# Rows turned by VectorE and exchanged in SBUF, and new orders in two stages of a four-layer graph network

## What is computed

```
x = _layernorm(x + L0(x))   # relu([x, max over edges of x[dst] - x[src]] @ W + b)
x = _layernorm(x + L1(x))   # silu(x @ lin), two convs with edge sums, cat, three residual layers, norm
x = _layernorm(x + L2(x))   # degree-normed sum of x @ W over edges and loops, relu
x = _layernorm(x + L3(x))   # weighted edge sum, layer norm, relu
```

## Time and profile before

| | |
|---|---|
| time, median of 3 runs | 5421.13 us (5409.99 to 5424.0) |
| the profiled execution's own time | 5410.58 us |
| its span, first to last instruction | 5408.9 us |
| busy: TensorE, VectorE, ScalarE, GpSimd | 78%, 79%, 67%, 75% of the span |
| TensorE's mean granted clock | 0.863 |

### The profile page before, as it was taken

The page is one execution under the profiler, slowest core; times in us unless marked ns, Lnnn a source line. Parts: engine busy times, 40 slices in busy tenths (PEclk is TensorE's granted clock), DMA queues, the critical chain, the costliest instruction groups (busy, mean ns, idle before and its releaser), DMA issues. The chain is left out here.

```text
span 5408.9 us, 82889 instructions
## 1 busy us (share of the span) xinstructions
PE 4223.2 (78%) x18435; PEld 2618.7 (48%) x18558; DVE 4247.1 (79%) x8746; ACT 3645.5 (67%) x9127; POOL 4062.4 (75%) x4129
## 2 busy tenths in 40 slices
PE   6999999999999978999999888888576745551000
PEld 3555555555555533444444588887454534440000
DVE  7888888888888746788788799999788854457776
ACT  3777777777777635666666688888688854446665
POOL 6788888888888777777777177777777767777777
PEclk9999999999999989999999999999655567665555
DMA  6877787777777646777777699999798967774443
GB/s 181 206 208 205 204 200 205 208 204 199 209 205 203 163 106 202 208 203 205 207 202 207 207 383 376 377 378 374 272 281 280 285 196 227 229 242 152 135 135 104
DMA packets 850458, 1213.29 MB, mean 224 GB/s; under 512 B 347599, under 2 KB 517001, under 8 KB 850215
## 3 DMA queue, kind: packets, MB, share of 16 engines
q1 hardware_dynamic: 744566, 1059.81, 61.4%
q0 software_dynamic: 100352, 149.23, 12.7%
q10 hardware_dynamic: 5296, 1.73, 0.1%
HBM read 648.60 MB, written 438.76 MB: 201 GB/s over the span
## 5 line engine op out<-in xcount | busy, mean ns | idle before, releaser
L847 ACT ACTIVATE p_s<-p_ps,cols 128x512 f32<-128x512 f32 x588 | 404.5, 688 | 341.1 <-PE p_ps L801 216.7
L729 POOL DMA_INDIRECT home<-edge_row_cols,scatter_cols x392 | 447.1, 1141 | 119.3 <-issue 119.3
L198 POOL DMA_INDIRECT out<-u_res,scatter_cols x392 | 407.7, 1040 | 121.7 <-issue 118.4
L1196 POOL DMA_INDIRECT ring_rows<-t_rows,home_cols x384 | 409.1, 1065 | 119.2 <-issue 88.5
L191 POOL DMA_INDIRECT u_rows<-t_rows,home_cols x392 | 388.2, 990 | 145.5 <-issue 117.3
L191 POOL DMA_INDIRECT ring_rows<-t_rows,home_cols x400 | 396.7, 992 | 126.3 <-issue 114.7
L722 POOL DMA_INDIRECT p_xs<-in_x,src_cols x388 | 387.0, 997 | 123.3 <-issue 117.0
L722 POOL DMA_INDIRECT p_xd<-in_x,dst_cols x388 | 398.3, 1027 | 107.2 <-issue 107.2
L1205 POOL DMA_INDIRECT home_cols<-home,src_cols x376 | 368.1, 979 | 144.2 <-issue 86.0
L212 DVE BATCH_NORM_STATS2 r_counts<-r_v 128x6 f32<-128x256 f32 x980 | 373.4, 422 | 11.0 <-issue 0.9
L227 ACT ACTIVATE r_x<-r_v,r_nm,r_rs 128x128 f32<-128x128 f32 x784 | 321.8, 482 | 83.0 <-DVE r_nm L1773 83.0
(11 more groups left out here) (307 smaller groups left out, 13894.1 us busy)
## 6 DMA issues: line engine op xcount, KB each, us to landing
ring_rows<-in_x SPq DMA_DIRECT2D x98, 512.0 KB, 6.2
p_xT<-p_xt SPq DMA_DIRECT2D x392, 128.0 KB
t_rows<-p_o SPq DMA_DIRECT2D x98, 512.0 KB
p_x1T<-p_oT SPq DMA_DIRECT2D x392, 128.0 KB
hT<-ring_own SPq DMA_DIRECT2D x98, 512.0 KB
q_hn<-hT SPq DMA_DIRECT2D x98, 512.0 KB
r_h<-hT SPq DMA_DIRECT2D x98, 512.0 KB
r_x<-t_rows SPq DMA_DIRECT2D x98, 512.0 KB
```

Of the source, the lines that this page charges most:

```text
L198: nc.gpsimd.indirect_dma_start(out=table, out_offset=bass.IndirectOffsetOnAxis(ap=idx[:, j:j + 1], axis=0), in_=rows[:, j, :], in_offset=N ...
L729: nc.gpsimd.indirect_dma_start(out=tab["home"], out_offset=bass.IndirectOffsetOnAxis(ap=s["scat"][:, k:k + 1], axis=0), in_=s["at"][:, k:k ...
L847: nc.scalar.activation(act_out[i][:, :], flat(bank_r if i else bank_t), ACT.Silu, bias=col(LS0 + i)).then_inc(r_act[i], 1)
L1196: nc.gpsimd.indirect_dma_start(out=rows[:, e % 4, j, :], out_offset=None, in_=tab["t1"], in_offset=bass.IndirectOffsetOnAxis(ap=s["home"][ ...
```

## The change

In `setup`, a second half of layer 0's weights is loaded with its rows in the squares' order (`w1_swapped`), and `wsum` is the sum of the two swapped halves, made after the last weights have landed.

In `nodes01`:

- The target rows of an edge block are no longer turned by TensorE and copied by ScalarE. VectorE turns them in squares into one buffer (`p_xdt`), SyncE exchanges them with four DMAs of 64 KB into `p_xdT`, whose runs are 32 elements (128 bytes) long, and the edge products read that.
- TensorE's node products of layer 0 (794) move ahead of the two root products (784, 787).
- VectorE's line 952 moves behind the norm statistics of the step and behind residual 1; the new turning stands right after it.
- On GpSimd, four of the last index gathers (`homes(3)`) move behind the gathers of the first two edge blocks of the next stage.

In `edges1`:

- SyncE's loop first stores the finished block, loads the `ends` rows and issues the exchange `q_xT`, and then does the dense loads and the rest. The two loads of the `home` table move behind the first exchange.
- Residual product 0 goes to the bank `bank_t` in place of `bank_r`, so that it does not wait for ScalarE's read of residual product 2; that wait moves to residual product 1.

```diff
+                e = t // 2 - 1 - BEHIND
+                if live(e, EB):
+                    sp.wait_ge(xd_squared, e + 1)
+                    after(sp, e_product, e - 1)
+                    swap_groups(sp, xdT[:, e % 2].rearrange("p j a i -> p a j i"), xd_turned[:, :, :], xdT_in[e % 2])
...
-            homes(3)
...
+            homes(3)
...
+                if t.live(NB):
+                    q = t.pair()
+                    pe.wait_ge(xT_in[q.of(2)], landed(2, q, 4))
+                    after(pe, biased, t.b)
+                    for j in range(G):
+                        i = nc.tensor.matmul(bank_o[:, j, :], xT[:, q.of(2), j, :, :, t.slot % 2].rearrange("p a i -> p (a i)"), first["w0"][:, :],
+                                             start=True, stop=True)
+                    i.then_inc(product, 1)
                 n = t.back(7)
...
-                    pe.wait_ge(xd_copied, e.b + 1)
+                    pe.wait_ge(xdT_in[e.of(2)], landed(2, e, 4))
...
-                if even and e.live(EB):
-                    pe.wait_ge(xd_in[e.of(2)], landed(2, e, G))
-                    after(pe, xd_copied, e.b)
-                    transpose4(nc, bank_t, xd[:, e.of(2)], s["ident"]).then_inc(xd_turned, 1)
...
-                    nc.scalar.activation(xdT[:, e.of(2), :], flat(bank_t), ACT.Copy).then_inc(xd_copied, 1)
...
+                if even and e.live(EB):
+                    dve.wait_ge(xd_in[e.of(2)], landed(2, e, G))
+                    if e.past(1):
+                        dve.wait_ge(xdT_in[e.back(1).of(2)], landed(2, e.back(1), 4))
+                    turn_squares(nc, xd_turned[:, :, :].rearrange("p c (j i) -> p c j i", j=G), xd[:, e.of(2)]).then_inc(xd_squared, 1)
...
             for t in range(EB + 10):
+                e = t - 6
+                if live(e, EB):
+                    sp.wait_ge(r_added[2], e + 1)
+                    sp.dma_start(tab["eT"][e], hs[3][:, e % 4, :]).then_inc(h_saved[e % 4], DMA)
...
+                if t % 2 == 0 and live(t, EB):
+                    q = t // 2
+                    sp.wait_ge(squared, t + 2)
+                    after(sp, lined_g, t - 2)
+                    swap_groups(sp, xT[:, q % 2], squares[:, q % 2], xT_in[q % 2])
...
-                    after(pe, r_act[2], n.b)
-                    nc.tensor.matmul(flat(bank_r), s["lins"][:, 0, :], hs[0][:, n.of(2), :],
+                    if t.fixed and t.b == MASK_AT + 1:
+                        pe.wait_ge(copied, 2)
+                    nc.tensor.matmul(flat(bank_t), s["lins"][:, 0, :], hs[0][:, n.of(2), :],
...
                     pe.wait_ge(r_added[0], n.b + 1)
+                    after(pe, r_act[2], n.b)
```

More of the change, by code:

```diff
@@ L582, in nodes01 @@
         act_out = [sb(f"p_s{i}", [P, BLK]) for i in range(3)]
-        run, xdT = sb("p_run", [P, 2, BLK]), sb("p_xdT", [P, 2, BLK])
+        run, xd_turned, xdT = sb("p_run", [P, 2, BLK]), sb("p_xdt", [P, 4, BLK // 4]), sb("p_xdT", [P, 2, G, 4, 32])
         ve, oe, oeT = sb("p_ve", [P, 2, G, H]), sb("p_oe", [P, 2, G, H]), sb("p_oeT", [P, 2, BLK])
@@ L598, in nodes01 @@
         x_squared, xT_in = sem("x_squared"), [sem(f"xT_in{i}") for i in range(2)]
+        xd_squared, xdT_in = sem("xd_squared"), [sem(f"xdT_in{i}") for i in range(2)]
         (product, biased, summed, counted, guarded, rooted, scaled,
@@ L788, in step @@
                                      start=True, stop=True).then_inc(u_done2, 1)
[L789 to L796, removed]
                 n = t.back(8)
@@ L962, in step @@
                     residual(1, n)
+                q = t.pair().back(1)
+                if even and q.live(QB):
+                    lo, hi = batch(q)
+                    dve.wait_ge(rooted, q.b + 1)
+                    after(dve, applied, 2 * (q.b - 1), NB)
+                    after(dve, e_applied, q.b - 1 - BEHIND)
+                    nc.vector.scalar_tensor_tensor(nm[:, q.of(2), lo:hi], st[:, q.of(2), lo:hi, MEAN_OF], -1.0,
+                                                   rs[:, q.of(2), lo:hi], ALU.mult, ALU.mult).then_inc(scaled, 1)
+                if even and e.live(EB):
[3 more added lines that the diff above has]
+                    turn_squares(nc, xd_turned[:, :, :].rearrange("p c (j i) -> p c j i", j=G), xd[:, e.of(2)]).then_inc(xd_squared, 1)
                 if not even and e.live(EB):
@@ L1132, in _ @@
             home_v = tab["home"].rearrange("(b p h) o -> p b (h o)", p=P, h=2 * G)
-            for c in range(NC):
-                sp.dma_start(home[:, c].rearrange("p (b h) j -> p b (h j)", h=2),
-                             home_v[:, c * NB // 4:(c + 1) * NB // 4, :]).then_inc(home_in[c], DMA)
             for t in range(EB + 10):
+                e = t - 6
+                if live(e, EB):
+                    sp.wait_ge(r_added[2], e + 1)
+                    sp.dma_start(tab["eT"][e], hs[3][:, e % 4, :]).then_inc(h_saved[e % 4], DMA)
+                e = t - 3
+                if e % 2 == 0 and live(e, EB):
+                    after(sp, masked, e - 2)
+                    load_row_pair(sp, ends[:, e % 4:e % 4 + 2, :], tab["ends"], e // 2, ends_in[e // 2 % 2])
+                if t % 2 == 0 and live(t, EB):
[3 more added lines that the diff above has]
+                    swap_groups(sp, xT[:, q % 2], squares[:, q % 2], xT_in[q % 2])
+                if t == 0:
+                    for c in range(NC):
+                        sp.dma_start(home[:, c].rearrange("p (b h) j -> p b (h j)", h=2),
+                                     home_v[:, c * NB // 4:(c + 1) * NB // 4, :]).then_inc(home_in[c], DMA)
                 if t == DENSE_AT:
```

43 lines of the change are left out of this document (9 added, 34 removed).

## The result

The changed kernel takes 5363.55 us in the median (5357.78 to 5371.38) against 5422.57 for the kernel before; the ratio is 0.9901, with a 95% interval of 0.9878 to 0.9924. The forecast was 5330, its range 5304 to 5398. The direction holds and the time lies in the range, but about a third of the gain is missing. The profiled execution has a span of 5357.8 us against 5408.9. The stages divide the difference of 51.1 us like this; each point of time is the start of an instruction in the two traces.

The account below looks back on a forecast made before the run. TensorE was taken to bound `nodes01`; 59 + 25 + 6 + 1 - 3 - 1 = 87 us off the profiled 5410.58 gives 5324, set at 5330 because the runs' median is higher. Range 5304 to 5398 (the forecast's own 5305 to 5350).

Parts of the forecast that it names:

- TensorE's sum a pair: `nodes01`: 18.64 us less 0.44 of turning and 0.36 of waits for `p_xx` gives 17.84 us a pair.
- the slack of 5.9 us from issue to use: Exchange `p_xdT` in `nodes01`: costs nothing up to 4.97 + 0.9 = 5.9 us; each microsecond beyond costs 92 us.
- The three waits in `edges1`: `edges1`, exchange issued first: three waits of 6.3 us go, plus 2 us each at half clock; 25 us, bounds 0 and 30.
- The other bank: `edges1`, residual product 0 in another bank: 0.07 us a step over about 85 steps, 6 us (0 to 17).
- 16.9 us of chain: `nodes01`: closed chain from edge products through VectorE, turning and exchange back to TensorE, 16.9 us, 0.9 under the 17.84 pair.
- the 59: `nodes01` gain: 92 pairs at 18.0 us, a little over TensorE's sum for stray waits, save 0.64 each; 59 us.
- the exchange is late: Rival at line 812, once a pair: at 7.5 us from issue to use, about 5460; no faster kernel, chance 0.10.
- its milder form: Exchange in `nodes01` a little late, 5.9 to 6.7 us from issue to use; time 5345 to 5390, chance 0.08.
- behind it on SyncE wait: SyncE in `nodes01`: `p_oeT` store, mask row and next `p_xT` follow the exchange, all needed a pair later; SyncE stays partly idle.
- the bound of 74: Upper bound of the `nodes01` gain, with no stray waits: 92 x 0.80 = 74 us.
- GpSimd's estimated pair of 17.6: `nodes01`: GpSimd's pair without delays, twelve issues with gaps about 15.1 us plus 2.5 for the power, about 17.6 us.
- the GpSimd rival: GpSimd sets the pace in `nodes01`: not under 18.4 us a pair, gain there 20 us, time about 5370; chance 0.14.

Follow-up runs that it names:

- `mid_side`: `mid_turn` with the 21 side transfers of SyncE issued one per iteration in place of in one go; 5317.86 us, ratio 0.9845 to the kernel before.
- `mid_turn`: Changed kernel, target rows turned in the odd step before, between residual 1 and the edge products' bias, exchanged ahead of store hT; 5322.13 us, ratio 0.9821.
- `order_only`: Kernel before with one edit, TensorE's node products of layer 0 ahead of the two root products; 5441.71 us against 5417.78, ratio 1.0059.
- `after`: The changed kernel itself in its first measurement; 5363.55 us against 5422.57 for the kernel before, ratio 0.9901.
- `after_again`: The changed kernel once more, unaltered; 5361.5 us (5352.83 to 5403.71).
- `nodes_only`: Changed kernel with the old function `edges1`; 5420.39 us against 5415.21 for the kernel before, ratio 1.001.

## Why the prediction was right and where it was wrong

**Right.** TensorE's sum a pair (17.84, measured 17.83). For the exchange, the slack of 5.9 us from issue to use (measured 5.90) and the ordinary duration ("5 to 5.5"; the landing median of 4.95 and 0.09 to the start make 5.04). Its packets: 12.8 ns each, 1.64 us of 16 engines, within 1.1 to 2.15. The three waits in `edges1` with the restart at half the clock (25 us, measured 25.3 over that stretch). The other bank (6 us, measured 3.1 over the steps from the 25th on: TensorE's step fell by 0.04 in the mean, not 0.07). The gathers at the end of `nodes01` (3 us, measured 3.5). In the set-up 0.2 us were lost, not 1.

**Wrong.** The step that failed is the exchange, costed at nothing because 16.9 us of chain lie 0.9 under the pair. The forecast set one isolated exchange against the slack. Both figures were right, but an exchange has no single duration: with a median of 4.95, a tenth of them took over 7.08 us, and 22 of 98 were later than they may be. TensorE had no idle time left in which to make a wait good, and the pair with the wait of 2.50 us took 20.49 in place of 17.83. The waits make 36.0 us in the profiled execution. That this equals the missing 59 - 23 = 36 is chance, since the 59 already held 92 x 0.16 = 15 us for stray waits. Against TensorE's bare sum, 74 - 23 = 51 us are missing. `mid_side`, which has no such wait, gets 48 of them back in this stage (1796.9 in place of 1845.0): the 36 us of waits and 12 more. About 8 of the 12 are TensorE's clock, as the kernel after shows behind the wait of 2.50 us (the timeline, and the windows view of the pair that begins there):

```profile
795.11 0.77 PE L817 MATMUL p_ps<-w_sum,p_xdT 128*128 128x128 f32 x2 [2.50 <-issue]
795.67 0.64 PE L818 MATMUL p_ps<-w_neg,p_run 128*128 128x128 f32 x2
796.10 0.63 PE L817 MATMUL p_ps<-w_sum,p_xdT 128*128 128x128 f32 x2
...
795.11:814.53 19.42, 19.42 (x69) 11.73 (x69) 14.60 (x26) 10.37 (x19) 13.50 (x12) 0.92 0.76 200
```

From line 818 to 817 it is 0.43 us in place of 0.22: these products run at 1.2 GHz, and the granted clock of the pair is 0.92. Behind the waits of 11.59, 2.13 and 2.53 us it is 0.89, 0.91 and 0.92. Waits at line 817 apart, these four pairs take 8 us more than the same pairs of `mid_side`. The rest is about 0.2 us beside each of the other waits.

The rival "the exchange is late" had the right place and price per microsecond, but I treated the lateness as a shift of all exchanges and not as a tail, and gave its milder form 0.08. The result lies in that form's 5345 to 5390, so it was luck that it fell into the stated range: that range took in this rival, while the forecast's own, 5305 to 5350, missed.

A second part of the same step: "behind it on SyncE wait" was asked, what stands ahead of the exchange on SyncE was not. The 21 side transfers cost 11.6 us there.

That this was the cause is shown by `mid_turn` and `mid_side`: with the exchange issued 7.5 us earlier the pair is 17.90, and with the side transfers spread the time is 5318, 100 us under the kernel before run beside it, where the forecast's sum was 87. The node stage then gains 71 us, close to the bound of 74.

**Right only with a move that was costed at nothing.** The forecast gave the new order of TensorE 0.36 us a pair by itself, and moving line 952 behind residual 1 was costed at nothing. `order_only` shows what the new order is worth with line 952 at its old place: a loss of 24 us. The kernel after has almost no such wait (2.1 us in all at its line 957, against 128.0 at line 952 in `order_only`). That the move alone is what saves it was not tried; the chain in `order_only` speaks for it. GpSimd's estimated pair of 17.6 is not reached in any run: in `mid_side` it goes round in 17.84 without waiting. Whether it could go faster is not shown. In the kernel before it was as full (between 900 and 1300 us no gap is over 0.35) and went round in 18.64; in `mid_side` its issues are shorter, the scatters 1.01 us in the mean in place of 1.15. So the GpSimd rival fell because its delays shrank, as the forecast had held against it.

**Open.** What holds up the late exchanges. For the one issued at 1086.78, the last packet is through after 4.28 us and 59 of 63 recorded landings are there by 4.39, but the last four come at 5.41, 7.35, 7.47 and 7.60. The Trainium skill, Perfetto Trace Analysis, section DMA Instruction — HWDGE, says that each DMA engine writes the semaphore only after its previous write is confirmed, and that this can take surprisingly long. Data that is through while a few landings are missing agrees with that. But it is so in about half of the late exchanges of the kernel after: in 10 of 22 the data is through within 4.5 us, in 10 others it takes over 5 us itself.

The traces narrow the search. I took exchanges 4 to 96 of the three kernels with the same node stage (`after`, `after_again`, `nodes_only`). Where SyncE takes over 2.85 us to issue the four DMAs (2.65 to 2.72 in most), 28 of 37 exchanges are late. Of the others, 58 of 123 are late where GpSimd issues the first of its scatters (line 736) up to 3.1 us behind the exchange's first issue, and none of 119 where it does so later. So the late ones come where GpSimd stands early in its pair against the exchange. That is a coincidence in time: no run moved the scatters, and GpSimd's gathers move with them. Which engine or which other transfer it is, no run here shows.

## What to carry to other kernels

When a wait moves onto the bounding engine with little time to spare, compare the slack with the late tail of the transfer, not with one isolated transfer or a median, and look at what stands ahead of it on its queue at every point of the stage, side work too. If the operand is ready earlier, issue the transfer earlier: here 7.5 us more slack were worth more than any change of the neighbours or the packets. An edit that takes a wait off the bounding engine can lose when a second engine is as full as the first; look who holds the pace next before pricing it.

## What the runs showed of the hardware

- A late tail of landings: four DMAs of 64 KB each from SBUF to SBUF land in 4.95 us in the median and in up to 8.50, at an engines' share of 0.90, and the number of late ones is 22, 28 and 41 of 98 in three kernels with the same code in the stage.
- Weights read with a stride of 16 bytes take twice as long: 0.47 us from one product to the next in place of 0.22, while line 791, which reads at a stride of 8 bytes, takes its four products in 0.94 us. VectorE's turning that writes with 16 bytes of stride takes 1.13 in place of 0.70. The Trainium skill, SBUF — State Buffer, section Door 1: The DMA port swizzle (why `[64,N]` ≈ `[32,N]`), says that accesses within one 16-byte line are fast and each that crosses to a new line pays; both rows agree, with the penalty already at a stride of four fp32.
- GpSimd's indirect DMA takes from 0.94 us to issue (the shortest in `mid_side`) to 1.46 (in `order_only`), and GpSimd's pair from 17.84 to 19.0 us, with the same instructions. The issue of 1.46 in `order_only` starts 0.03 us behind VectorE's line 907, which has two operands in SBUF, as the one of 1.32 in the earlier trace rows ran beside line 944; no run isolates this from what else differs.
- After waits of 2.13 to 11.59 us TensorE's granted clock over the next pair was 0.89 to 0.92 in the kernel after; after one of 2.98 us in `nodes_only` it stayed at 1.00.
